# Splitting the filler between two transpose turns of an attention kernel: half a value product and half a projection piece in every step

## The chip, the cores and the metric

The program runs on one core of a Trainium2 chip. The time is the device time of one execution in microseconds (us); lower is better. Traces come from one profiled execution.

## What is computed

Two layers over x of shape 8 x 512 x 32 x 32, each added to its input. Only the first one is touched by the change. Cut to what matters:

```python
xs = group_norm(x).reshape(b, c, seq).transpose(0, 2, 1)      # 1024 pixels, 512 channels
qkv = xs @ Wqkv + bqkv
q, k, v = heads(qkv)                                          # 8 heads of 64
scores = einsum('bhqd,bhkd->bhqk', q, k) / sqrt(64)
attn = softmax(scores)
out = einsum('bhqk,bhkd->bhqd', attn, v)
x = x + (out.reshape(b, seq, c) @ Wout + bout)
```

The second layer (deformable attention in windows of 8 x 8 pixels) works on the result.

## The kernel before, in words

Every engine's program is written out by hand in its order, with semaphores between them. The outer loop goes over the 8 images (`i`). Inside it the attention of the first layer is cut into 32 steps (`n`, `STEPS`): four pairs of heads (`PAIRS`) times eight tiles of 128 queries (`KT`). Work of the second layer for the image before is spread over some of the steps; the rest of it, the output projection and so on follow behind step 31.

In step n TensorE (PE) does this, in this order:

1. `scores(n + 1)` (line 647): 12 matmuls of 64 rows x 512 columns, three products of the high and low halves of q and k for two heads side by side. They need the exponentials of step n to have freed both score banks.
2. `turn(n, 0)` (line 663): 8 transposes of the first head's exponentials into the banks `TB`, which ScalarE (ACT) then copies to `exps_turned` (line 1097).
3. a filler: a value product or a projection piece.
4. `turn(n, 1)`: 8 transposes of the second head's, which VectorE (DVE) copies (line 1425). They wait until ACT has emptied `TB`.

The filler is what the change touches. `value_product(u, half, i)` (line 678) multiplies the turned exponentials of two steps with the values into the bank `OB`; two halves of 16 matmul instructions each in the trace, of 128 rows x 64 columns of weights, two heads side by side. `keep_output` (ACT, line 1201) copies `OB` away. `piece(n, i)` (line 618) computes 512 columns of the next pair's q or k into the bank `MB` with 12 matmuls of 128 rows x 128 columns of weights; ACT (`high_piece`, line 1077) and DVE (`low_piece`, line 1409) split it into halves in `QK`. There are 12 pieces for each image, for n = 0, 2, ..., 22. Their weights stand in a ring of two slots, `wqk_ring`, which the DMA queue of SyncE refills (`load_wq`, line 461) behind the transfers of the reciprocals.

The filler before: step 0 and all odd steps up to 21 hold a whole piece; even steps from 2 to 20 hold a whole value product; steps 22 to 31 hold half a product each.

ACT does in a step: `copy_turned(n)`, the two exponentials of step n + 1 (line 1087), and `keep_output` or `high_piece` if there is one. DVE does two row maxima (line 1416), `copy_turned`, and `low_piece` if there is one. Between them they also hold small work of the second layer; at n = 4 ACT computes a logarithm, for which it loads another table, and loads the table of the exponential again in step 5.

Of the kernel before, what the change touches and what calls it, by code (L numbers as in the profile page):

```python
# [14 lines left out]
CT = C // P  # L15
# [20 lines left out]
def piece_of(n):  # L36
    p, j = n // KT + 1, n % KT
    return (p, j // 2) if p < PAIRS and j % 2 == 0 else None
# [39 lines left out]
def build(nc, x, wqkv, bqk, bv, wo0, bo0, lnw, lnb, lnwt, lnbt, wqT, wkT, wvT, woT, bo1, dww, dwb, pwT,  # L78
          w1T, b1, w2T, b2, w3c, b3, c_ident, c_gavg, c_gxy, c_grid, out):
    with ExitStack() as ctx:  # L80
# [3 lines left out]
        def sem(name):  # L84
            return ctx.enter_context(nc.semaphore(name))

        def at(name, shape, offset, dt=F32):
            return nc.alloc_sbuf_tensor_at(name, shape, dt, offset=offset)
# [44 lines left out]
        WQ = at("wqk_ring", [P, 2, 2, CT, P], AT_WQ, F32R)  # L133
# [82 lines left out]
        MB = PS[:, 7]  # L216
# [64 lines left out]
        piece_full = sem("piece_full")  # L281
# [88 lines left out]
        def wait_after(eng, s, count):  # L370

            if count > 0:
                eng.wait_ge(s, count)
# [223 lines left out]
        def _(pe):  # L597
# [17 lines left out]
            def project_halves(dst, weights, c, ks):  # L615
                for k in ks:
                    for a, half in ((0, XH), (0, XL), (1, XH)):
                        mm = pe.matmul(dst, weights[:, a, k], half[:, k, c:c + 512], start=(k == 0 and a == 0 and half is XH),  # L618
                                       stop=(k == CT - 1 and a == 1))
                return mm  # L620
# [46 lines left out]
            def value_product(u, half, i):  # L667
                p = u // 4
                if half == 0:
                    pe.wait_ge(t_free[0], i * STEPS + 2 * u + 2)  # L670
                    pe.wait_ge(t_free[1], i * STEPS + 2 * u + 2)
                    wait_after(pe, ob_kept, i * (OUTS - 1) + u)
                    if u == 0 and i:
                        pe.wait_ge(off_done, i)
                for kt in range(4 * half, 4 * half + 4):
                    for h in range(2):
                        hc = (2 * p + h) * D
                        mm = pe.matmul(OB[D * h:D * h + D, 0:256], V[:, kt, hc:hc + D], PT[:, u % 2, h, kt],  # L678
                                       start=(kt == 0), stop=(kt == KT - 1))
                if half == 1:  # L680
                    mm.then_inc(av_full, 1)
# [9 lines left out]
                                       skip_group_check=True)  # L691
                mm.then_inc(rbc_full, 1)

            def piece(n, i):
                p, which = piece_of(n)
                w, c = which // 2, 512 * (which % 2)
                pe.wait_ge(wq_in[w], 16 * (PAIRS * i + p))
                wait_after(pe, piece_free, (i * 3 + p - 1) * PIECES + which)
                if n == 0 and i >= 2:
                    pe.wait_ge(o1c_done, i - 1)  # L700
                project_halves(MB, WQ[:, w], c, range(CT)).then_inc(piece_full, 1)

            def group_sums(k, dst, after=0):
                pe.wait_ge(gn_in, k)
# [52 lines left out]
            def turn_sampled(f, j):  # L757
                pe.wait_ge(kvt_done, 2 * j + f + 1)
                turn_rows().then_inc(kv_full, 1)
# [205 lines left out]
            for i in range(B):  # L965
                for n in range(STEPS):
                    if n + 1 < STEPS:
                        scores(n + 1, i)
                    turn(n, 0, i)
                    if n == 0:  # L970
                        piece(0, i)
                    if n >= 2 and n % 2 == 0:
                        value_product(n // 2 - 1, 0, i)
                    if (2 <= n < 22 and n % 2 == 0) or (n > 22 and n % 2):
                        value_product(n // 2 - 1, 1, i)
                    if piece_of(n + 1):
                        piece(n + 1, i)
                    if i + 1 < B and n == STEPS - 1:
                        values(0, i + 1)
                    if i and n == 25:  # L980
                        turn_sampled(0, i - 1)
                    if i and n == 26:
                        turn_sampled(1, i - 1)
                    if i and n == 28:
                        turn_similarities(0, i - 1)
                    if i and n == 29:
                        turn_similarities(1, i - 1)
                    turn(n, 1, i)
                    if i and n == 1:
                        offsets(i - 1)  # L990
                    if i and n == 23:
                        turn_weights(i - 1)
                    if i and n == 24:
                        sample(0, i - 1)
                    if i and n == 25:
                        sample(1, i - 1)
                    if i and n == 26:
                        sampled_keys(i - 1)
                    if i + 1 < B and n == 26:
                        group_sums(2 * i + 2, GSO)  # L1000
                    if i and n == 27:
                        similarities(0, i - 1)
                    if i and n == 28:
                        similarities(1, i - 1)
                    if i and n == 30:
                        sampled_values(i - 1)
                spread_recips(i)
                for half in range(2):
                    value_product(OUTS - 1, half, i)
                if i + 1 < B:  # L1010
                    values(1, i + 1)
                pe.wait_ge(wo0_in, 16 * (i + 1))
                for t in range(CT):
                    project(("o0", t, i), WO0, P * t, OTH, OTL, needs=attended if t == 0 else None)
                if i + 1 < B:
                    values(2, i + 1)
                group_sums(min(2 * i + 3, 2 * B), GSM, i)
                if i + 1 < B:
                    values(3, i + 1)
                if i:  # L1020
                    mlp(i - 1, i)
                else:
                    for n in range(4):
                        pixels(n, i)
                    first_pair(0, 1)
                    first_pair(1, 1)
                    channel(0, i)
                for t in range(1, CT):
                    channel(t, i)
                if i:  # L1030
                    turn_bias(i - 1)
                queries(i)
                if i:
                    if i + 1 < B:
                        first_pair(0, i + 1)
                    attend(i - 1)
                    if i + 1 < B:
                        first_pair(1, i + 1)
                    apply_values(i - 1)
                    for t in range(3):  # L1040
                        output(t, i - 1)
                if i + 1 < B:
                    scores(0, i + 1)
                if i:
                    output(3, i - 1)
# [20 lines left out]
        def _(act):  # L1066
# [173 lines left out]
            for i in range(B):  # L1240
                for h in range(2):
                    exp(0, h, i)
                for n in range(STEPS):
                    if i + 1 < B and n == 22:
                        next_image(i + 1)
                    if i and n in (25, 26):
                        keep_sampled(n - 25, i - 1)
                    if i and i + 1 < B and n == 26:
                        act.dma_start(WV[:].bitcast(F32), wv_dram).then_inc(wv_in, 16)
                    if i and n in (28, 29):  # L1250
                        keep_similarities(n - 28, i - 1)
                    copy_turned(n, i)
                    if n + 1 < STEPS:
                        for h in range(2):
                            exp(n + 1, h, i)
                    if (2 <= n < 22 and n % 2 == 0) or (n > 22 and n % 2):
                        keep_output(n // 2 - 1, i)
                    if i + 1 < B and n in (27, 28):
                        x_high(2 * (n - 27), i + 1)
                        x_high(2 * (n - 27) + 1, i + 1)  # L1260
                    if n == 0:
                        high_piece(0, i)
                    if piece_of(n + 1):
                        high_piece(n + 1, i)
                    if i and n == 0:
                        gelu(i - 1)
                    if i and n == 1:
                        tanh(i - 1)
                    if i and n == 4:
                        log(i - 1)  # L1270
                    if not i and n in (4, 10):
                        wo_high(n // 10)
# [662 lines left out]
```

## Time and profile before

| what | value |
|---|---|
| median of 3 runs | 3384.9 us (3383.76 to 3387.4) |
| profiled execution, its own time | 3384.37 us |
| its span in the trace | 3382.4 us |
| PE busy | 3177.9 us (94%) |
| DVE busy | 2276.8 us (67%) |
| ACT busy | 1689.2 us (50%) |

Times in the trace count from the start of the span. An instruction of TensorE has two records, the weight load (PEld) and the matmul (PE). Matmuls overlap and their ends are modelled, so the distance from start to start tells how long a group took; a busy PE can hide a short gap between two groups.

### The profile page before, as it was taken

The page shows a single profiled execution, that of the slowest core. Times are in us where ns is not written, and L with a number is a line of the kernel's source. Part 1 is how long each engine was busy: PE and PEld are TensorE (multiplying, and loading weights), DVE is VectorE, ACT ScalarE, POOL GpSimd, SP SyncE. Part 2 cuts the span into 40 slices and gives each one's busy share as a digit, 9 for nine tenths or more (in the row PEclk, how much of TensorE's full clock was granted, in tenths as well). Part 3 has the DMA queues.
Part 4 walks back from the last instruction along what each step waited for, and adds up shares of the span by engine and source line. Part 5 has one row for each costly group of instructions (what it writes and reads, how often), then busy time and mean ns, then how long its engine had stood idle before and what let it go on. Part 6 is the DMA issues. An engine that isn't in the chain of part 4 may idle for free.

```text
span 3382.4 us, 51739 instructions
## 1 busy us (share of the span) xinstructions
PE 3177.9 (94%) x20704; PEld 2250.2 (67%) x20704; DVE 2276.8 (67%) x3031; ACT 1689.2 (50%) x2500; POOL 220.9 (7%) x165
## 2 busy tenths in 40 slices
PE   6999699999999999999999999999999999998978
PEld 5767576657766677666776567675776757765545
DVE  5666567677676676776666866668667576666765
ACT  2553455364553655444653645537455364553533
POOL 0000020000100020000200002000020000200200
PEclk9999899999999999999999999999999999998979
DMA  5222012301133111321123111221113311103121
GB/s 180 66 79 80 14 38 76 118 32 43 34 76 113 38 39 40 108 74 53 32 59 99 55 63 31 67 98 39 64 34 79 97 49 48 34 11 118 38 59 50
DMA packets 132158, 213.24 MB, mean 63 GB/s; under 512 B 76561, under 2 KB 95508, under 8 KB 128052
## 3 DMA queue, kind: packets, MB, share of 16 engines
q1 hardware_dynamic: 127252, 182.68, 17.4%
q10 hardware_dynamic: 4672, 27.26, 2.7%
q8 instruction: 168, 2.75, 0.5%
q14 instruction: 66, 0.54, 0.1%
HBM read 162.40 MB, written 47.50 MB: 62 GB/s over the span
## 4 chain that ended last, share of the span: by engine, by line
PE 79%; DVE 11%; ACT 4%; issue 3%; DMA 2%; SPq 0%; another core or an unknown queue 0%; POOL 0%; DVEq 0%; ACTq 0%
PE banks L663 13%; PE banks L678 13%; PE banks L647 11%; PE banks L618 9%; PE banks L608 8%; PE banks L719 4%; PE banks L850 4%; PE banks L860 3%; PE banks L851 3%; PE banks L852 3%; ACT exps L1087 2%; DVE qk_halves L1592 2%; PE banks L926 2%; PE banks L823 2%; DVE neg_max L1416 1%
## 5 line engine op out<-in xcount | busy, mean ns | idle before, releaser
L1416 DVE TENSOR_REDUCE neg_max<-banks 128x1 f32<-128x1024 f32 x512 | 601.6, 1216 | 70.4 <-PE banks L647 68.3
L1425 DVE COPY exps_turned<-banks 128x1024 f32<-128x1024 f32 x256 | 313.5, 1224 | 496.8 <-PE banks L663 488.9
L1087 ACT ACTIVATE exps<-banks,neg_max 128x1024 f32<-128x1024 f32 x512 | 565.0, 1112 | 152.6 <-DVE neg_max L1416 151.3
L1097 ACT ACTIVATE exps_turned<-banks 128x1024 f32<-128x1024 f32 x256 | 262.4, 1025 | 685.9 <-PE banks L663 685.8
L663 PE MATMUL banks<-ident,exps 128*128 128x128 f32 x4096 | 552.3, 278 | 42.7 <-DVE exps_turned L1425 41.9
L663 PEld LDWEIGHTS banks<-ident,exps 128*128 128x128 f32 x4096 | 449.1, 141 | 197.6 <-issue 156.1
L678 PE MATMUL banks<-exps_turned,values 128*64 128x256 f32 x4096 | 483.3, 386 | 6.2 <-issue 6.2
L647 PE MATMUL banks<-qk_halves 64*128 64x512 f32 x3072 | 428.1, 410 | 52.3 <-ACT exps L1087 43.9
L678 PEld LDWEIGHTS banks<-exps_turned,values 128*64 128x64 f32 x4096 | 284.1, 137 | 156.6 <-issue 37.2
L647 PEld LDWEIGHTS banks<-qk_halves 64*128 64x128 f32 x3072 | 280.4, 186 | 137.3 <-issue 99.5
L1592 DVE SCALAR_TENSOR_TENSOR qk_halves<-banks,qk_halves 128x1024 fp32r<-128x1024 f32 x256 | 301.8, 1219 | 70.0 <-ACT qk_halves L1134 69.8
L618 PE MATMUL banks<-x_hi,wqk_ring 128*128 128x512 f32 x992 | 337.2, 403 | 0.0
L1134 ACT ACTIVATE qk_halves<-banks 128x1024 fp32r<-128x1024 f32 x256 | 249.2, 1022 | 143.9 <-PE banks L831 143.7
L850 PE MATMUL banks<-qk_halves,mlp_w_hi 128*128 128x512 f32 x512 | 233.7, 456 | 20.0 <-ACT exps L1150 13.8
L1608 DVE TENSOR_SCALAR exps<-banks,mlp_b 128x512 f32<-128x512 f32 x256 | 190.4, 746 | 33.7 <-PE banks L852 27.0
L618 PEld LDWEIGHTS banks<-x_hi,wqk_ring 128*128 128x128 f32 x992 | 186.6, 188 | 38.3 <-issue 1.7
L850 PEld LDWEIGHTS banks<-qk_halves,mlp_w_hi 128*128 128x128 f32 x512 | 98.5, 192 | 168.5 <-ACT exps L1150 117.8
L851 PE MATMUL banks<-qk_halves,mlp_w_hi 128*128 128x512 f32 x512 | 206.4, 403 | 0.0
L852 PE MATMUL banks<-qk_halves,mlp_w_lo 128*128 128x512 f32 x512 | 205.4, 401 | 0.0
L618 PE MATMUL banks<-x_lo,wqk_ring 128*128 128x512 f32 x496 | 193.8, 391 | 0.0
L1150 ACT ACTIVATE exps<-banks,mlp_b 128x512 f32<-128x512 f32 x256 | 168.1, 693 | 32.6 <-PE banks L852 32.4
L719 PE MATMUL banks<-wv_halves,x_hi 128*128 128x512 f32 x512 | 162.7, 399 | 10.6 <-DVE x_lo L1387 10.6
(189 smaller groups left out, 3899.6 us busy)
## 6 DMA issues: line engine op xcount, KB each, us to landing
wo_halves<-wo_split_dram SPq DMA_DIRECT2D x16, 2048.0 KB, 7.8
wqk_ring<-wqk_split SPq DMA_DIRECT2D x62, 512.0 KB, 4.3
exps_turned<-in_x SPq DMA_DIRECT2D x32, 512.0 KB, 5.3
x_dram<-exps SPq DMA_DIRECT2D x32, 512.0 KB, 2.6
exps_turned<-x_dram SPq DMA_DIRECT2D x32, 512.0 KB, 5.7
out<-exps_turned SPq DMA_DIRECT2D x32, 512.0 KB, 2.6
recips_b<-recips_dram SPq DMA_DIRECT2D x240, 64.0 KB, 3.8
x_image<-in_x ACTq DMA_DIRECT2D x14, 1024.0 KB, 14.4
```

Of the source, the lines that this page charges most:

```text
L618: mm = pe.matmul(dst, weights[:, a, k], half[:, k, c:c + 512], start=(k == 0 and a == 0 and half is XH), stop=(k == CT - 1 and a == 1))
L647: mm = pe.matmul(slot(("s", 2 * n + h, i))[:, 512 * c:512 * c + 512], QK[rows, p % 2, a, P * j:P * j + P], QK[rows, p % 2, b, 512 * c:512 ...
L663: mm = pe.transpose(TB[:, kt // 4, kt % 4 * P:kt % 4 * P + P], PB[:, 2 * h + n % 2, kt * P:(kt + 1) * P], IDENT[:])
L678: mm = pe.matmul(OB[D * h:D * h + D, 0:256], V[:, kt, hc:hc + D], PT[:, u % 2, h, kt], start=(kt == 0), stop=(kt == KT - 1))
L719: mm = pe.matmul(slot(("v", n, i))[:, 512 * s:512 * s + 512], half[:, k, P * tt:P * tt + P], WV[:, a, k], start=(k == 0 and half is XH and ...
L850: pe.matmul(h2_bank(c), W2H[:], h1_hi_half(u)[:, cols], start=True, stop=False)
L851: pe.matmul(h2_bank(c), W2H[:], h1_lo_half(u)[:, cols], start=False, stop=False)
L852: pe.matmul(h2_bank(c), W2L[:], h1_hi_half(u)[:, cols], start=False, stop=True)\
L1087: freed(act.activation(PB[:, 2 * h + n % 2], slot(("s", m, i)), ACT.Exp, bias=NM[:, m:m + 1], accum_out=SS[:, m:m + 1]), ("s", m, i))
L1416: dve.tensor_reduce(NM[:, m:m + 1], slot(("s", m, i)), AX.X, ALU.max, negate=True).then_inc(mx, 1)
L1425: dve.tensor_copy(PT[:, n // 2 % 2, 1, :, P * j:P * j + P], TB.rearrange("p s (k q) -> p (s k) q", k=4)).then_inc(t_free[1], 1)
L1592: freed(dve.scalar_tensor_tensor(out=h1_lo_half(u), in0=slot(("h1", u, j)), scalar=0.0, in1=h1_hi_half(u).bitcast(F32), op0=ALU.max, op1=A ...
```

## The change

Every step from 3 on holds half a value product (even steps the first half, odd ones the second), and every step from 2 to 21 also half a projection piece: even steps begin the piece for n + 2, odd steps end the one for n + 1. Step 1 still holds a whole piece, and so does step 0. Steps from 22 on are as they were. `keep_output` moves with the second half of the product, from even steps to odd ones.

```diff
-            def piece(n, i):
+            def piece(n, i, parts=(0, 1)):
                 p, which = piece_of(n)
                 w, c = which // 2, 512 * (which % 2)
+                if parts == (1,):
+                    project_halves(MB, WQ[:, w], c, range(2, CT)).then_inc(piece_full, 1)
+                    return
                 pe.wait_ge(wq_in[w], 16 * (PAIRS * i + p))
                 wait_after(pe, piece_free, (i * 3 + p - 1) * PIECES + which)
                 if n == 0 and i >= 2:
                     pe.wait_ge(o1c_done, i - 1)
-                project_halves(MB, WQ[:, w], c, range(CT)).then_inc(piece_full, 1)
+                if parts == (0,):
+                    project_halves(MB, WQ[:, w], c, range(2))
+                else:
+                    project_halves(MB, WQ[:, w], c, range(CT)).then_inc(piece_full, 1)
...
                     if n >= 2 and n % 2 == 0:
                         value_product(n // 2 - 1, 0, i)
-                    if (2 <= n < 22 and n % 2 == 0) or (n > 22 and n % 2):
+                    if n >= 3 and n % 2:
                         value_product(n // 2 - 1, 1, i)
+                    if n >= 2 and piece_of(n + 2):
+                        piece(n + 2, i, (0,))
                     if piece_of(n + 1):
-                        piece(n + 1, i)
+                        piece(n + 1, i, (0, 1) if n == 1 else (1,))
...
-                    if (2 <= n < 22 and n % 2 == 0) or (n > 22 and n % 2):
+                    if n >= 3 and n % 2:
                         keep_output(n // 2 - 1, i)
```

On TensorE, in the first image, an even and an odd step of before (line 663 are the turns, 678 the value product, 618 the piece, 647 the scores; a row of 678 counts each of its matmuls once, the trace twice):

```order
L663 MATMUL banks<-ident,exps 128x128 x8
L678 MATMUL banks<-exps_turned,values 64x256 x16
L663 MATMUL banks<-ident,exps 128x128 x8
L647 MATMUL banks<-qk_halves 128x512 x12
L663 MATMUL banks<-ident,exps 128x128 x8
L618 MATMUL banks<-x_hi,wqk_ring 128x512
L618 MATMUL banks<-x_lo,wqk_ring 128x512
L618 MATMUL banks<-x_hi,wqk_ring 128x512 x2
L618 MATMUL banks<-x_lo,wqk_ring 128x512
L618 MATMUL banks<-x_hi,wqk_ring 128x512 x2
L618 MATMUL banks<-x_lo,wqk_ring 128x512
```

The same engine and steps of the changed kernel, one whole step from its first turn to the next scores:

```order
L663 MATMUL banks<-ident,exps 128x128 x8
L678 MATMUL banks<-exps_turned,values 64x256 x8
L618 MATMUL banks<-x_hi,wqk_ring 128x512
L618 MATMUL banks<-x_lo,wqk_ring 128x512
L618 MATMUL banks<-x_hi,wqk_ring 128x512 x2
L618 MATMUL banks<-x_lo,wqk_ring 128x512
L618 MATMUL banks<-x_hi,wqk_ring 128x512
L663 MATMUL banks<-ident,exps 128x128 x8
L647 MATMUL banks<-qk_halves 128x512 x12
```

Both the even and the odd step read so now: 8 of the 16 product matmuls and 6 of the 12 of the piece stand between the two turns, and the engine goes from the product straight to the piece.

On ACT, before, an even step and an odd one (1097 the copy of the turned exponentials, 1087 the exponentials, 1201 `keep_output`, 1077 `high_piece`):

```order
L1097 ACTIVATE exps_turned<-banks 128x8x128
L1087 ACTIVATE exps,exp_sums<-banks,neg_max 128x1024 x2
L1201 ACTIVATE attended<-banks 128x256
L1097 ACTIVATE exps_turned<-banks 128x8x128
L1087 ACTIVATE exps,exp_sums<-banks,neg_max 128x1024 x2
L1077 ACTIVATE qk_halves<-banks,b_qk 128x512
```

And with the change (8 lines further down in the file):

```order
L1105 ACTIVATE exps_turned<-banks 128x8x128
L1095 ACTIVATE exps,exp_sums<-banks,neg_max 128x1024 x2
L1105 ACTIVATE exps_turned<-banks 128x8x128
L1095 ACTIVATE exps,exp_sums<-banks,neg_max 128x1024 x2
L1209 ACTIVATE attended<-banks 128x256
L1085 ACTIVATE qk_halves<-banks,b_qk 128x512
```

`keep_output` now stands in the odd step, ahead of `high_piece`.

## Rows read from the trace of the kernel before

**Rows 1.** The page, busy time, share of the span and instructions.

```profile
PE 3177.9 (94%) x20704; PEld 2250.2 (67%) x20704; DVE 2276.8 (67%) x3031; ACT 1689.2 (50%) x2500; POOL 220.9 (7%) x165
```

**Rows 2.** Stretches of image 3: steps 2-21, 18, 19, 5, 22.

```profile
core 0: us, PE busy (x) PEld busy (x) DVE busy (x) ACT busy (x) POOL busy (x), PEclk, DMA share, GB/s
1215.95:1352.08 136.13, 134.94 (x1000) 99.99 (x1000) 87.09 (x113) 77.48 (x125) 20.31 (x16) 1.00 0.13 33
1325.10:1332.35 7.25, 7.25 (x62) 5.00 (x62) 4.14 (x4) 3.86 (x7) 0.00 (x0) 1.00 0.04 2
1332.35:1338.59 6.24, 6.24 (x42) 4.98 (x41) 3.98 (x5) 3.53 (x6) 0.00 (x0) 1.00 0.10 21
1236.65:1244.14 7.49, 6.31 (x41) 5.00 (x41) 6.62 (x11) 5.94 (x9) 0.00 (x0) 1.00 0.28 91
1352.08:1358.12 6.04, 5.59 (x45) 3.87 (x45) 4.55 (x5) 3.48 (x6) 0.00 (x0) 1.00 0.37 32
```

**Rows 3.** Timeline of PE, steps 18 and 19: start, us, line, operation.

```profile
1325.10 1.67 PE L647 MATMUL banks<-qk_halves 64*128 64x512 f32 x12
1326.70 1.09 PE L663 MATMUL banks<-ident,exps 128*128 128x128 f32 x8
1327.72 3.67 PE L678 MATMUL banks<-exps_turned,values 128*64 128x256 f32 x32
1331.32 1.09 PE L663 MATMUL banks<-ident,exps 128*128 128x128 f32 x8
1332.35 1.66 PE L647 MATMUL banks<-qk_halves 64*128 64x512 f32 x12
1333.93 1.09 PE L663 MATMUL banks<-ident,exps 128*128 128x128 f32 x8
1334.78 0.48 PE L618 MATMUL banks<-x_hi,wqk_ring 128*128 128x512 f32 x1
...
1337.62 1.03 PE L663 MATMUL banks<-ident,exps 128*128 128x128 f32 x8
1338.59 0.74 PE L647 MATMUL banks<-qk_halves 64*128 64x512 f32 x4
```

**Rows 4.** Timeline of PE, step 22 and the start of step 23.

```profile
1352.08 1.67 PE L647 MATMUL banks<-qk_halves 64*128 64x512 f32 x12
...
1354.70 1.95 PE L678 MATMUL banks<-exps_turned,values 128*64 128x256 f32 x16
1356.58 1.09 PE L663 MATMUL banks<-ident,exps 128*128 128x128 f32 x8
1358.12 1.66 PE L647 MATMUL banks<-qk_halves 64*128 64x512 f32 x12 [0.45 <-issue]
```

**Rows 5.** Timeline of PE, step 31: half product, then values of the next image.

```profile
1418.58 1.95 PE L678 MATMUL banks<-exps_turned,values 128*64 128x256 f32 x16
1420.46 0.74 PE L719 MATMUL banks<-wv_halves,x_hi 128*128 128x512 f32 x2
...
1421.95 0.61 PE L719 MATMUL banks<-wv_halves,x_hi 128*128 128x512 f32 x2
```

**Rows 6.** Timeline of ACT in step 5 of image 3.

```profile
1240.41 1.28 ACT L1087 ACT_TABLE_LOAD   x1
...
1243.80 0.20 ACT L1087 ACTIVATION_READ_ACCUMULATOR exps<-banks,neg_max 128x1 f32 x1
1243.89 0.69 ACT L1077 ACTIVATE qk_halves<-banks,b_qk 128x512 fp32r<-128x512 f32 x1
```

**Rows 7.** The instructions on the ring of weights: its loads, issue to landing.

```profile
DMA to landing us min/median/max: 3.1/4.3/13.6
```

**Rows 8.** Timeline of SyncE's queue and of PE in image 4, steps 5 and 6.

```profile
1644.96 0.58 SPq L461 DMA_DIRECT2D wqk_ring<-wqk_split  x1
1650.91 1.66 PE L647 MATMUL banks<-qk_halves 64*128 64x512 f32 x12 [1.19 <-ACT exps L1087]
```

**Rows 9.** Step 31 of image 2, its half product, as a stretch.

```profile
1009.71:1013.01 3.30, 3.30 (x17) 1.54 (x17) 0.13 (x1) 1.02 (x1) 0.00 (x0) 0.56 0.09 30
```

## The prediction

> **What bounds the kernel now.** I read the page first. TensorE is busy for 94% of the span, DVE and ACT far less [rows 1]. Then I cut the trace at the starts of the score groups, which gives the length of each step, and asked for the engines' busy time in these stretches. In image 3, steps 2 to 21 take 136.13 us and TensorE is busy for 134.94 of them; step 18, with a whole value product, takes 7.25 us and step 19, with a whole piece, 6.24, and in both TensorE is busy throughout [rows 2]. All images show these two lengths. A step with half a product and nothing else takes 6.04 us and has 0.45 us of idle time before its next scores [rows 4]: that is the time in which ACT and DVE can turn a step around. Both step lengths in question are above it. So steps 2 to 21 are bound by what TensorE issues, and not by the loop of scores, maxima, exponentials and copies. One step is an exception: step 5, 7.49 us with only 6.31 busy [rows 2], because ACT loads the table of the exponential again (1.28 us) before its exponentials; they end at 1243.80 + 0.20, and the next scores start at 1244.14 [rows 2, 6].
>
> Where PE is busy throughout, the question is what its groups cost, each from its start to the start of the next. The timeline gives it [rows 3]:
>
> - scores to turn: 1326.70 - 1325.10 = 1.60
> - turn to product: 1.02; turn to piece: 1334.78 - 1333.93 = 0.85
> - whole product to turn: 1331.32 - 1327.72 = 3.60
> - piece to turn: 1337.62 - 1334.78 = 2.84
> - second turn to scores: 1.03 after a product, 0.97 after a piece
>
> The reader is to see that the same 8 transposes cost 0.17 us more when a product follows than when a piece follows. Weights of the turns and of the piece fill 128*128 of the array, those of the product 128*64, those of the scores 64*128. Each change of this form costs something, and turn to piece is not such a change.
>
> **The change, part by part.** No matmul is added or removed: 32 product instructions and 12 of the piece for each pair of steps, before and after. What changes is the number of changes of form. Before, an even step has four (scores, turn, product, turn, scores) and an odd one two; with the change each step has four, since product to piece is one and piece to turn is none. That is two more for each pair of steps, in 10 pairs and 8 images.
>
> *Second product group:* two halves in place of a whole. A half costs 1356.58 - 1354.70 = 1.88 [rows 4] and the same before a group of form 128*128 with 512 columns: 1420.46 - 1418.58 = 1.88 [rows 5]. So 2 x 1.88 - 3.60 = +0.16.
> *Turn to product in the odd step too:* 1.02 - 0.85 = +0.17.
> *The piece in two parts:* six instructions of the same shape behind a half product take 1421.95 - 1420.46 = 1.49 [rows 5], two times that is 2.98, against 2.84: +0.14.
> *Second turn behind a piece in both steps:* 0.97 in place of 1.03: -0.06.
> Sum +0.41 a pair. Added up as a whole step, 1.60 + 1.02 + 1.88 + 1.49 + 0.97 = 6.96, a pair 13.92 against 13.49, +0.43; the difference is rounding, and I take 0.42, so 6.955 a step.
>
> The Trainium skill has the rule behind this, in "TensorEngine Tiling (Array Packing)", section Key Properties: changing the tiling mode drains TensorE. It speaks against the change and gives no figure; the rows bear it out, with about 0.2 us for each change (0.42 for two more). By the view that only matmuls count, the pair would stay at 13.49.
>
> *Step 5* stays at 7.49, set by ACT, as its own TensorE work of 6.96 is still below it. So here the longer filler costs nothing, while step 4 gets shorter. In an image, steps 2 to 21 become 20 x 6.955 + (7.49 - 6.955) = 139.6, against 136.13: +3.5. Image 0 has no such table load but other waits of the kind; I take it as equal. 8 x 3.5 = +28.0 us.
>
> *Waits that come with it, even steps:* the first half of a piece now needs `MB` and its weights at 1.60 + 1.02 + 1.88 = 4.50 us into an even step, where before they were needed 1.60 + 0.85 = 2.45 us into the odd step behind it. `MB` is freed by `low_piece`, behind DVE's copy of the step before. All five DVE instructions of step 19 take 3.98 us [rows 2], and this one stands second of those that come after the turn; it is done before 4.50, and I cost it at nothing. If that cover were gone, everything behind it on TensorE (second turn, next scores) would move, one for one.
> *The ring of weights:* this cover is thinner. In image 4, a load is issued at 1644.96 and step 6 starts at 1650.91 [rows 8]. Now it is wanted at 1650.91 + 4.50 = 1655.4; with the median landing of 4.3 it lands at 1649.3, with the longest of 13.6 [rows 7] at 1658.6: 3.2 us late. Before, it was wanted at 1650.91 + 7.25 + 2.45 = 1660.6, and even the longest was in time. 4 loads an image are of this kind. At best none is late (0), at worst a few of the 32 are late by some 3 us (10 us). Since the median is 6 us early, the value is nearer to the lower end: +4.
> *`keep_output`* moves to odd steps, between the exponentials and `high_piece`. ACT is busy for 3.86 and 3.53 us in steps of 7.25 and 6.24 [rows 2], so it has room; the next product starts in the next even step, 2.6 us after its scores, and these already need the exponentials that stand before `keep_output`. Nothing.
> *Steps 0, 1 and 22 to 31 and all behind them* are untouched. TensorE's clock matters at one place there: the half product of step 31 took 3.30 us in image 2 at a granted clock of 0.56 [rows 9], against 1.88 in image 3 [rows 5], the engine having waited just before it. Where the low stretch (1.2 of 2.4 GHz) falls can move with the rest; each gained or lost is 1.4 us, and I count none, some 6 us for the range.
>
> **The sum.** 3384.37 (the profiled execution's own time; its span is 3382.4) + 28.0 + 4 = 3416.4. The median of the runs is 3384.9, 0.5 above, within their own spread. I say 3416.
>
> **The rivals.**
>
> *The even filler removes a wait (faster).* The idea: a step with a short filler is bound by the others' loop, one with a long filler by TensorE, and the mean of both fillers is better than their alternation. For it speaks that the odd step, 6.24, is only 0.20 above the loop of 6.04. The mechanism decides from the point where a short step is longer than its TensorE work; the saving is then what it waits. If TensorE's busy time hid 0.3 us of such a wait in each odd step, and the changes of form were free besides, a pair would be 13.19: 80 x -0.3 = -24, 3360 us. Against it: 6.24 of 6.24 busy, and turn to piece, piece to turn add up without a gap. Chance 0.04.
>
> *Nothing happens.* The groups' overlap hides the changes of form when the groups are small. Then only step 4 against 5 counts; 7.25 and 7.49 become 6.75 and 7.49: 8 x -0.5 = -4, and with the ring's +4 it is 3384. Against it are the half products of rows 4 and rows 5, which show the 0.08 each. Chance 0.04.
>
> *A new wait in the even step.* `MB` or the ring is late not now and then but each time, as the first half piece is wanted a step earlier. At 0.5 us for each of the 80 even steps it is +40 on top of 28: 3453; if only the ring's loads are later than I take, with 10 to 20 us in place of 4, 3422 to 3432. For it speaks the landing of up to 13.6; against it 3.98 before 4.50 and the median landing. It begins where a load takes more than 10.4 us from its issue (1655.4 - 1644.96). Chance 0.10.
>
> *As worked out:* 0.82, with its own range from 3404 (no late load, 6 us less by the clock, 0.35 a pair) to 3428 (10 us of late loads, 6 of the clock).
>
> **How the numbers follow.** 3403 to 3430 holds the likely case and the milder part of the third rival; outside it lie the first two rivals (0.08) and the harder part of the third, so about 0.15 in all. A measurement of this kernel tells some 0.2% (7 us) from no change. Slower by more than that: 0.82 + 0.10 = 0.92. Within: 0.05, the second rival and the edge of the first. Faster: 0.03.
>
> **What the profile of the changed kernel would show.** Step lengths from scores to scores of 6.95 us, even and odd alike, in steps 2 to 21 but for step 5 near 7.5; each made of 1.60, 1.02, 1.88, 1.49 and 0.96. The same counts of matmuls; TensorE still busy throughout. No wait before the first half piece but in a few steps, where a load of the ring landed late; these would show as idle time of PE ended by the ring's DMA. Steps 22 to 30 as before. I am wrong if the even step waits for `low_piece` throughout, if product to piece costs less than the 0.08 and 0.07 that the halves show, or if odd steps come out under 6.9.

## The result, and the profile after

The changed kernel takes 3428.05 us (median of 6 runs, 3418.51 to 3438.74); the kernel before, in the runs beside it, 3386.15 (3382.19 to 3390.82). The ratio is 1.0122, with a 95% interval of 1.0099 to 1.0145: the change makes the kernel slower by 1.2%. The profiled execution took 3424.17 us (span 3422.2), 39.8 more than the profiled one of before.

The page shows the same number of matmuls, and TensorE busy for 3218.4 us where [rows 1] had 3177.9, 40.5 more; the other engines' busy times hardly differ:

```profile
PE 3218.4 (94%) x20704; PEld 2249.2 (66%) x20704; DVE 2280.8 (67%) x3031; ACT 1687.0 (49%) x2500; POOL 221.7 (6%) x165
```

The busy time of the engines in stretches of image 3, cut again at the starts of the score groups: steps 2 to 21 together, then steps 18, 19, 5 and 22. They answer to [rows 2, 4]. Step 2 is among them: it too holds half a product and half a piece now.

```profile
core 0: us, PE busy (x) PEld busy (x) DVE busy (x) ACT busy (x) POOL busy (x), PEclk, DMA share, GB/s
1229.48:1371.86 142.38, 139.20 (x1000) 99.26 (x1000) 87.81 (x113) 77.45 (x125) 20.43 (x16) 1.00 0.12 32
1344.05:1351.00 6.95, 6.95 (x51) 4.95 (x50) 4.15 (x4) 3.21 (x5) 0.00 (x0) 1.00 0.00 0
1351.00:1357.96 6.96, 6.96 (x53) 4.96 (x52) 3.98 (x5) 4.15 (x7) 0.00 (x0) 1.00 0.09 19
1250.34:1257.84 7.50, 7.02 (x51) 4.98 (x51) 5.92 (x11) 5.71 (x9) 0.00 (x0) 1.00 0.31 91
1371.86:1377.90 6.04, 5.59 (x45) 3.85 (x45) 4.56 (x5) 3.21 (x5) 0.00 (x0) 1.00 0.28 29
```

Steps 18 and 19, 7.25 and 6.24 before, are now 6.95 and 6.96, and TensorE is busy in all of both. Step 5 is 7.50 and step 22 is 6.04, as before. But the 20 steps take 142.38 us with 139.20 busy: 3.2 us are idle, where before 1.2 were (7.49 - 6.31 in step 5). Of these 3.2, step 5 has 0.5, so 2.7 lie elsewhere. The timeline of TensorE shows step 18 by its groups, beside [rows 3]:

```profile
1344.05 1.66 PE L647 MATMUL banks<-qk_halves 64*128 64x512 f32 x12
1345.64 1.09 PE L663 MATMUL banks<-ident,exps 128*128 128x128 f32 x8
1346.66 1.95 PE L678 MATMUL banks<-exps_turned,values 128*64 128x256 f32 x16
1348.54 0.50 PE L618 MATMUL banks<-x_hi,wqk_ring 128*128 128x512 f32 x1
...
1350.04 1.04 PE L663 MATMUL banks<-ident,exps 128*128 128x128 f32 x8
1351.00 0.50 PE L647 MATMUL banks<-qk_halves 64*128 64x512 f32 x2
```

From start to start: 1.59 scores, 1.02 turn before a product, 1.88 half product, 1.50 half piece, 0.96 second turn: 6.95. The same timeline in step 14 of the same image shows the gap:

```profile
1316.08 1.95 PE L678 MATMUL banks<-exps_turned,values 128*64 128x256 f32 x16
1320.73 0.50 PE L618 MATMUL banks<-x_hi,wqk_ring 128*128 128x512 f32 x1 [2.70 <-DMA wqk_ring<-wqk_split]
```

The half product would have made room for the half piece at 1316.08 + 1.88 = 1317.96; the weights of the ring came at 1320.7. SyncE's queue just before:

```profile
1305.77 1.08 SPq L476 DMA_DIRECT2D recips_b<-recips_dram  x2
1306.96 3.12 SPq L485 DMA_DIRECT2D mlp_rows<-attended  x4
1310.13 0.59 SPq L461 DMA_DIRECT2D wqk_ring<-wqk_split  x1
```

The load was issued at 1310.13, behind the reads of the reciprocals and the four transfers of `rows_to_dram`, 7.8 us ahead of the time at which it was wanted, and took 10.6 us to land.

A late load can cost more than the wait for it. In step 10 of image 5 (2111.05 to 2121.32) TensorE waited for the load as well, and in this step the granted clock is 0.86:

```profile
2117.54 0.50 PE L618 MATMUL banks<-x_hi,wqk_ring 128*128 128x512 f32 x1 [1.93 <-DMA wqk_ring<-wqk_split]
...
2111.05:2121.32 10.27, 8.35 (x51) 5.88 (x50) 4.47 (x5) 3.21 (x5) 0.00 (x0) 0.86 0.06 14
```

The first matmul comes 2.0 us late, but the step is 3.32 us longer than 6.95, and step 11 behind it (clock 0.96) is 0.27 longer. In image 3 the engine waited longer, 2.7 us, and the clock in that step stayed at 1.00; so a wait doesn't bring a low clock each time.

**Where the 39.8 us are**, from the lengths of all steps in the two traces:

| part | us |
|---|---|
| steps 2 to 21, length of the steps without a late load | +27.1 |
| steps 2 to 21, three steps with a late load, with the low clock in the last (image 0 step 10 +1.85, image 3 step 14 +2.78, image 5 step 10 +3.32) | +7.95 |
| steps 22 to 29 | +3.7 |
| all behind step 30 of the images | +0.6 |

The four numbers sum to 39.4; the other 0.4 lie in the start and in steps 0 and 1. In steps 22 to 29 there are two things. In step 22 of image 5 (7.87 us in place of 6.04) ACT took 2.32 us to issue one of the two loads of the next image; in the kernel before none of the 14 issues took more than 0.49. And step 26 takes 11.27 in place of 9.64 us in images 1 and 5, at a granted clock of 0.85; in the kernel before it is 1.00 in step 26 of every image. Image 0, on the other hand, has 0.7 us less in step 26 than before.

TensorE's busy time in steps 2 to 21 grew by some 4.2 us in each image but image 5 (134.94 to 139.20 in image 3), more than the 3.5 of the steps' length: step 5 is set by ACT, and 0.7 us of its idle time were filled. In image 5 it grew by 5.9, since busy time counts the low clock too.

### The profile page after: what moved, and what is told of

Same layout as the page of the kernel before. It is cut to its first block, busy times and chain, and to the rows that moved or that the text cites. A ratio compares the mean times of both kernels' runs of the same rounds, so it can differ in the third digit from the quotient of the medians.

```text
span 3422.2 us, 51739 instructions
## 1 busy us (share of the span) xinstructions
PE 3218.4 (94%) x20704; PEld 2249.2 (66%) x20704; DVE 2280.8 (67%) x3031; ACT 1687.0 (49%) x2500; POOL 221.7 (6%) x165
## 4 chain that ended last, share of the span: by engine, by line
PE 78%; DVE 11%; ACT 4%; issue 3%; DMA 3%; SPq 0%; another core or an unknown queue 0%; ACTq 0%; POOL 0%; DVEq 0%
PE banks L663 12%; PE banks L678 12%; PE banks L647 10%; PE banks L618 10%; PE banks L608 8%; PE banks L725 4%; PE banks L856 4%; PE banks L866 3%; PE banks L857 3%; PE banks L858 3%; DVE qk_halves L1600 2%; PE banks L932 2%; PE banks L829 2%; ACT exps L1095 2%; DVE neg_max L1424 1%
## 5 line engine op out<-in xcount | busy, mean ns | idle before, releaser
L663 PEld LDWEIGHTS banks<-ident,exps 128*128 128x128 f32 x4096 | 457.7, 142 | 178.3 <-issue 154.5
L678 PE MATMUL banks<-exps_turned,values 128*64 128x256 f32 x4096 | 503.7, 389 | 6.2 <-issue 6.2
L618 PE MATMUL banks<-x_hi,wqk_ring 128*128 128x512 f32 x992 | 361.8, 415 | 6.4 <-DMA wqk_ring<-wqk_split 6.4
L856 PE MATMUL banks<-qk_halves,mlp_w_hi 128*128 128x512 f32 x512 | 233.9, 457 | 20.3 <-ACT exps L1158 13.5
L725 PE MATMUL banks<-wv_halves,x_hi 128*128 128x512 f32 x512 | 161.7, 397 | 10.6 <-DVE x_lo L1395 10.6
```

The costliest lines, as they stand in the source:

```text
L663: mm = pe.transpose(TB[:, kt // 4, kt % 4 * P:kt % 4 * P + P], PB[:, 2 * h + n % 2, kt * P:(kt + 1) * P], IDENT[:])
L725: mm = pe.matmul(slot(("v", n, i))[:, 512 * s:512 * s + 512], half[:, k, P * tt:P * tt + P], WV[:, a, k], start=(k == 0 and half is XH and ...
L856: pe.matmul(h2_bank(c), W2H[:], h1_hi_half(u)[:, cols], start=True, stop=False)
```

## Experiments

The theory A to be tested: each change of the weights' form on TensorE (128*128, 128*64 or 64*128 of the array) costs about 0.2 us, the change adds two for each pair of steps, and that is 27 us; what is beyond is loads of the ring that are wanted earlier than before, and come late. Rival B: it is the cutting into halves that costs (fill, new banks, more groups), or the new order of product and piece, whatever the forms. Rival C: the loads of the ring are all there is to the even steps' growth.

**The ring's load ahead of the reciprocals.** On the kernel after:

```diff
                 for u in range(OUTS - 1):
+                    if u in (1, 3, 5, 7):
+                        load_wq(4 + u // 2, i)
                     recips_around(u, i)
...
-                    if u in (1, 3, 5, 7):
-                        load_wq(4 + u // 2, i)
```

> The changed kernel, with the four loads of the ring of weights of each image issued one transfer of reciprocals earlier (ahead of it in SyncE's queue in place of behind it), some 10 us. Theory A (the loss is the changes of form on TensorE, about 28 us, and on top of it loads of the ring that land late, 8 us in the profile of the changed kernel and more in its slower runs): the step lengths stay at 6.95, no wait for the ring is left, the time is 3384.4 + 28 = 3412 to 3416 and the runs lie closer together than 3418 to 3439. Rival B (the late loads are a by-product and something else spreads the runs): time and spread as in the changed kernel, about 3428.

Measured: 3416.38 us (3414.77 to 3422.41), with 3412 to 3416 expected, beside 3393.54 of before on the same chip, 1.0069 (1.0057 to 1.0082). The 62 loads still take up to 13.6 us. The view of all that touches `wqk_ring` has no transfer any more among what TensorE waited for. In the kernel after it had 6 such waits, 14.2 us: 3 late loads, each counted at a matmul and at a weight load.

```profile
L461 SPq DMA_DIRECT2D wqk_ring<-wqk_split x62: 319/583/2821, 45.5 to 2967.8; - x62
its engine sat idle before it (us, times) until:
  issue: 64.4, 172
...
DMA to landing us min/median/max: 3.1/4.5/13.6
```

In images 2 to 4 the load is now issued 22 to 26 us ahead of its use, in place of 6.7 to 11.6. Steps 2 to 21 are +26.9 us against before, all at 6.95 (but for step 5, and step 11 of image 0). So the ring's part goes away with the early load, and the 27 us stay: C falls.

**The same pair side by side on a second chip**, since the result's 1.0122 and this 1.0069 were not measured beside each other. The kernel after, unchanged:

> The changed kernel itself, beside the kernel before and the other three on one chip. Theory A: even and odd steps of 6.95, one to five waits for the ring of weights in the even steps 6, 10, 14 and 18, of 1 to 4 us each; 30 to 45 us above the kernel before.

3438.23 us (3429.7 to 3444.52), 1.0135 (1.0113 to 1.0156). With the early load:

> The changed kernel with the ring's loads issued ahead of a transfer of reciprocals, once more, now beside the changed kernel itself. Theory A: no wait for the ring, 27 us of longer steps left; 20 to 30 us above the kernel before, and 8 to 18 us below the changed kernel. Rival B (the ring's loads are no cause of their own): within 4 us of the changed kernel.

3419.41 us (3415.69 to 3422.99), 1.0080 (1.0066 to 1.0094): 19 us below, on one chip (4 runs of each, whose ranges don't meet). In the trace of the unchanged kernel the same view of the ring's loads reads

```profile
  DMA wqk_ring<-wqk_split: 28.0, 12
...
DMA to landing us min/median/max: 3.1/4.7/13.8
```

and steps 2 to 21 are +47.4 us against before, of which 27 are the steps' length and 20.3 late loads and what follows them: six steps wait for a load (one to five were expected), in images 0, 1, 3, 4 and 5, and the longest takes 12.20 us in place of 6.95. TensorE's matmuls wait 12.6 us for loads in all. Most of the other 7.7 goes with a lower granted clock: four of the six steps, and the step behind one of them, have 0.79 to 0.89 in place of 1.00. With the early load no step from 2 to 21 has a lower clock, and these steps are +26.8. The two traces of the kernel after have three and six late loads. That this number changes between executions would explain why its runs spread over 20 and 15 us, and those with the early load over 8 and 7; it was not counted in the runs without a trace.

**The same edit of the load, on the kernel before:**

> The kernel before, with the ring's loads issued early in the same way. Theory A: in the kernel before even the longest landing (13.6 us) is in time, so nothing is gained: within 3 us of the kernel before. Rival B (loads issued early help in any case, by another order in SyncE's queue): faster by 8 us or more.

3389.90 us (3385.6 to 3398.59) beside 3391.27, 0.9999 (0.9989 to 1.0010). A load took up to 14.5 us there, and none was late. The early load gives nothing by itself; it takes back what late loads had added to the changed kernel. Expectation and prediction both say that in the kernel before even the longest landing is in time. That is so at step 6 of image 4, but in the trace of before the load of step 10 of image 0 was issued only 10.0 us ahead of its use, and that of step 14 of image 1 10.3. They landed after 7.5 and 4.0; with 13.6 they would have been late.

**Product in halves, piece whole.** On the kernel after:

```diff
-                    if n >= 2 and piece_of(n + 2):
-                        piece(n + 2, i, (0,))
                     if piece_of(n + 1):
-                        piece(n + 1, i, (0, 1) if n == 1 else (1,))
+                        piece(n + 1, i)
```

> One part of the change alone: the product is held in halves by even and odd steps, but the piece stays whole in the odd step. Theory A: the even step has 1.60 + 1.02 + 1.88 + 1.03 = 5.53 us of TensorE work, which is below the 6.04 that the loop of maxima, exponentials and copies takes, so it takes 6.04 and waits 0.5; the odd step takes 1.60 + 1.02 + 1.88 + 2.87 + 0.97 = 8.34. A pair 14.38, 80 x 0.89 = +71 us, about 3455. Rival D (unequal steps cost nothing, as the loop has slack elsewhere): 5.53 + 8.34 = 13.87, as the changed kernel, about 3416.

One run, 3457.79 us, where about 3455 was expected. Busy times of an odd and an even step of it:

```profile
1365.94:1374.25 8.31, 8.31 (x57) 6.19 (x57) 3.52 (x5) 4.18 (x7) 0.00 (x0) 1.00 0.13 16
1374.25:1380.32 6.07, 5.58 (x45) 3.85 (x45) 4.60 (x5) 3.21 (x5) 0.00 (x0) 1.00 0.01 3
```

The even step has only 5.58 us of matmuls and takes 6.07, with its next scores waiting for the exponentials:

```profile
1380.32 0.96 PE L647 MATMUL banks<-qk_halves 64*128 64x512 f32 x6 [0.49 <-ACT exps L1093]
```

Here is the loop of scores, maxima, exponentials and copies that the prediction gave 6.04 us. No even step of 2 to 21 goes below 6.03, and what the odd step gets on top adds in full. Of the divisions that were run this is the one in which an uneven filler has a price, and the kernel before was not it: its short step, 6.24, was above the loop.

**Three changes of form in place of four.** On the kernel with the early load, the half product of steps 2 to 21 goes behind the second turn, so that turn, half piece, turn stand together:

```diff
                     turn(n, 1, i)
+                    if 2 <= n < 22:
+                        value_product(n // 2 - 1, n % 2, i)
```

with the two calls between the turns kept for n >= 22 alone.

> As the run before it, but in steps 2 to 21 the half product stands behind the second turn, just ahead of the next scores, and only the half piece stands between the turns. Every step holds the same matmuls as in the changed kernel, but changes the form of the weights three times in place of four (scores to turn, turn to product, product to scores; the piece has the turns' form), six for a pair, as many as the kernel before. Theory A (each change of form costs about 0.2 us): steps of 1.60 + 0.85 + 1.46 + 0.97 + 1.88 = 6.76, a pair 13.52 against 13.49 of before, the time within 4 us of the kernel before (3382 to 3390). Rival C (what costs is that the groups are smaller, or that each step has both fillers): steps stay at 6.95 and the time at 3412 or more. A wait of the second turn for ACT's copy would show as longer steps too: by the rows it is done 2.2 us after the first turn starts, and wanted at 2.31.

3404.79 us (3401.0 to 3411.17), 1.0035 (1.0023 to 1.0048), 11 us above before where at most 4 were expected. The step's length came as expected and the total did not. TensorE's timeline of a step:

```profile
1327.40 1.65 PE L647 MATMUL banks<-qk_halves 64*128 64x512 f32 x12
1328.98 1.09 PE L663 MATMUL banks<-ident,exps 128*128 128x128 f32 x8
1329.83 0.48 PE L618 MATMUL banks<-x_hi,wqk_ring 128*128 128x512 f32 x1
...
1331.31 1.04 PE L663 MATMUL banks<-ident,exps 128*128 128x128 f32 x8
1332.28 1.95 PE L678 MATMUL banks<-exps_turned,values 128*64 128x256 f32 x16
1334.16 1.21 PE L647 MATMUL banks<-qk_halves 64*128 64x512 f32 x8
```

6.76 us, as worked out, with both the product and the piece in halves and the same matmuls. The pair is 13.54 against 13.49 before and 13.91 in the kernel after; steps 2 to 21 of all images together are 1.1 us *below* before. (Step 4 got shorter while step 5 is still set by ACT.) So halves have hardly a price in themselves, 0.05 us a pair, and B's first half falls. What makes this kernel slower than before lies elsewhere: in its trace steps 22 to 29 are +22.7 us. ACT's timeline in step 22 of image 3, and the stretches of steps 22 and 23:

```profile
1356.20 4.10 ACTq L1228 DMA_DIRECT2D x_image<-in_x  x2
1360.40 1.02 ACT L1107 ACTIVATE exps_turned<-banks 128x1024 f32<-128x1024 f32 x1 [4.84 <-issue]
```

```profile
1354.48:1363.71 9.23, 5.62 (x46) 3.85 (x45) 4.05 (x4) 4.17 (x7) 0.00 (x0) 1.00 0.44 31
1363.71:1371.35 7.64, 7.58 (x49) 5.62 (x50) 3.40 (x6) 3.37 (x6) 0.00 (x0) 0.78 0.70 258
```

ACT issues the two loads of the next image for 4.1 us; its copy of the turned exponentials is behind them, TensorE waits for that (5.62 of 9.23 busy), and in the step behind, the granted clock is 0.78 and the step takes 7.64 in place of 6.07. It happened in three of the seven images (3.69 us the longest single issue), and the low clock in step 23 in two of these. Step 22 of the three is 8.1 us longer in all and step 23 3.1; step 26 of images 3, 4 and 5 has the low clock (11.27 in place of 9.64), 4.9 in all. The rest is in images 0 (+4.0, with step 26 at a clock of 0.73) and 7 (+3.0).

**The same, with that issue placed behind the exponentials.** On top of the last one:

```diff
-                    if i + 1 < B and n == 22:
-                        next_image(i + 1)
...
                             exp(n + 1, h, i)
+                    if i + 1 < B and n == 22:
+                        next_image(i + 1)
```

> The kernel with three changes of form in each step and the ring's loads early, with one more edit: ACT issues the load of the next image in step 22 behind its copy and exponentials in place of ahead of them. In its last profile that kernel won 1 us against the kernel before in steps 2 to 21 and lost 23 in steps 22 to 29: in images 3, 4 and 5 the issue took 2.5 to 3.7 us in place of 0.5 while the copy waited behind it, and stretches of low clock fell into steps 23 and 26. Theory A: with the issue behind ACT's urgent work, step 22 is 6.04 in all images, low clock in step 23 is gone, and the time comes within 5 us of the kernel before on the same chip. Rival E (the low clock in steps 22 to 29 comes by itself, from where the images' lengths put it): step 22 is 6.04, but steps 23 or 26 keep their longer forms, and the time stays 5 to 10 us above. Either way there is no clear gain on the kernel before.

3387.76 us (3383.17 to 3398.11) beside 3390.92, 0.9993 (0.9981 to 1.0006): no difference from before. ACT's timeline:

```profile
1355.44 1.02 ACT L1107 ACTIVATE exps_turned<-banks 128x1024 f32<-128x1024 f32 x1 [1.64 <-PE banks L663]
1356.36 1.11 ACT L1097 ACTIVATE exps<-banks,neg_max 128x1024 f32<-128x1024 f32 x1
1356.89 1.71 ACTq L1228 DMA_DIRECT2D x_image<-in_x  x2
```

The issue now lies beside the exponential, and step 22 takes 6.03 to 6.05 in all images. The low clock in step 23 is gone as well. But step 26 still has a granted clock of 0.85 in images 1, 2 and 6 (11.25 to 11.27 us), and steps 22 to 29 are +6.0 in the trace: rival E was right about step 26. Its 5 to 10 us in the total did not come. So with halves, three changes of form a step, early loads and the later issue, the even filler costs nothing that the runs tell from before, and brings nothing. No version that I ran is faster than before.

**One more change of form in the kernel before, with the piece untouched.** The second half of the product goes behind the second turn in the even steps:

```diff
-                    if (2 <= n < 22 and n % 2 == 0) or (n > 22 and n % 2):
+                    if n > 22 and n % 2:
                         value_product(n // 2 - 1, 1, i)
...
                     turn(n, 1, i)
+                    if 2 <= n < 22 and n % 2 == 0:
+                        value_product(n // 2 - 1, 1, i)
```

> The kernel before, with one edit: in the even steps 2 to 20 the second half of the value product stands behind the second turn in place of ahead of it. Pieces, and the work of each step, are as before; the even step has five changes of form in place of four. Theory A: even steps take 1.60 + 1.02 + 1.88 + 1.03 + 1.88 = 7.41 in place of 7.25, odd ones 6.24 as before; 80 x 0.16 = +13 us, 3397 to 3400. Rival C (groups that hold both fillers cost, a change of form is free): 3384, no change. A gain would mean that the copies of ACT and DVE were late for the turns before.

3413.30 us (3408.29 to 3416.16), 1.0054 (1.0040 to 1.0068).

```profile
1339.62 1.66 PE L647 MATMUL banks<-qk_halves 64*128 64x512 f32 x12
1341.22 1.09 PE L663 MATMUL banks<-ident,exps 128*128 128x128 f32 x8
1342.24 1.95 PE L678 MATMUL banks<-exps_turned,values 128*64 128x256 f32 x16
1344.12 1.09 PE L663 MATMUL banks<-ident,exps 128*128 128x128 f32 x8
1345.14 1.95 PE L678 MATMUL banks<-exps_turned,values 128*64 128x256 f32 x16
```

The even step is 7.39 (expected 7.41), the odd one 6.26: a product in halves with a turn between them costs 0.14 to 0.16 us more than whole, with all else as before. That is what A gives, and the price is on TensorE. The total was expected at +13 and measured at +20, which is a miss. In image 0 the steps 5, 6, 11 and 12 grew (8.28 and 8.95 in place of some 7.25), 5.5 us of the 17.6 in steps 2 to 21. At the end of step 5 TensorE waits 1.95 us for the exponentials, where before 0.94: ACT's `keep_output` has to wait for the moved half, and both it (101.81 in place of 100.97) and the exponentials (107.49 in place of 106.65) come 0.84 us later. In the steps behind (6 and 12) the granted clock is 0.81. And step 26 of images 2 to 6 fell in a low clock. One of them, from this kernel's trace, and the same stretch from the kernel before:

```profile
1393.00:1404.20 11.20, 8.78 (x77) 5.96 (x66) 7.81 (x21) 3.81 (x6) 0.00 (x0) 0.85 0.69 241
```

```profile
1378.66:1388.30 9.64, 7.22 (x62) 5.45 (x58) 7.89 (x20) 3.81 (x6) 0.00 (x0) 1.00 0.64 221
```

A granted clock of 0.85 in place of 1.00, and 1.6 us more.

**Piece ahead of product.** On the kernel with the early load, the two lines of the piece stand ahead of those of the product, so that the changes of form are as many (four a step) but in another order.

> The changed kernel with early loads of the ring and, in steps 2 to 21, the half piece ahead of the half product. Four changes of form as in the changed kernel (scores to turn, piece to product, product to turn, turn to scores). Theory A: steps of 6.95 as there, within 0.05, and no wait. If it is the step from product to piece that costs and not any change of form, the steps come out near 6.76.

One run, 3405.30 us. From start to start a step is 1.59 scores, 0.84 turn, 1.57 half piece, 1.88 half product, 1.02 second turn: 6.90. The order of product and piece is worth 0.05 us a step; the four changes keep the rest (6.76 with three). B's second half falls too, except for these 0.05. By these two kernels the fourth change costs 0.14 us, by the changed kernel and the one with three 0.19. What in the change of form takes this time, no run takes apart.

## Why the prediction came out as it did

**The step lengths: right, and not by luck.** Predicted 6.955 even and odd, step 5 at 7.49; measured 6.95 and 7.50, by 1.59, 1.02, 1.88, 1.50 and 0.96 in place of 1.60, 1.02, 1.88, 1.49 and 0.97. The sum over steps 2 to 21 is 27.1 us of the +28.0 foretold; image 0, which the prediction took as equal, got 2.6 without its late load, as its steps 5 and 11 were bound by others before and got no longer. The experiments bear out the reason: one change of form more (+0.14 in the even step), four a step (6.95, 6.90 in the other order), three a step (6.76). Two more changes for each pair of steps are 0.37 us of the pair's 0.42 (13.91 - 13.54); the halves by themselves, without more changes, are the other 0.05.

The Trainium skill states, in "TensorEngine Tiling (Array Packing)", section Key Properties, that changing the tiling mode drains TensorE. The runs agree that such a change costs time, with (13.91 - 13.54) / 2 = 0.19 us for each of the two changes by which a pair differs between the kernels with four and three a step; the draining itself is in no row.

**`MB` and `keep_output` at nothing: right.** No even step waits as such; step 18 is 6.95 of 6.95 busy.

**The ring at +4: the term that was too small.** It measured 8.0 us in the profiled execution (8.2 with the step behind), and on the second chip 19 between the medians with and without early loads. The step that failed: "4 loads an image are of this kind", with the margin of the load of step 6 of image 4 (10.4 us from issue to use, which the trace of after confirms) for all of them. The four aren't alike. The load of step 14 stands behind `rows_to_dram` on SyncE's queue, and is issued 6.3 to 10 us ahead of its use; in image 0 the load of step 10 has 5.5. With the longest landing of before, 13.6 us, such a load comes 4 to 8 us late and not 3.2, and shorter landings are late too: the two with short leads landed after 7.2 and 10.6 us. The third late load, in step 10 of image 5, is of the kind that the prediction had in mind, with 10.7 us ahead and 12.6 to land. In the trace of before the load of step 14 already had a shorter lead than those of steps 6 and 10 in images 2 to 4 (12.4 to 12.8 us to its use, 15.0 to 16.5 at step 6 and 14.7 to 15.6 at step 10). The term also had nothing for the granted clock behind a late load: 1.3 of the 3.3 us of step 10 of image 5, and most of 7.7 beyond 12.6 us of waits on the second chip. The rival "if only the ring's loads are later than I take", 3422 to 3432, had priced this, and the median of 3428.05 lies there; of the likely case only its upper end (3428) reaches it. So the stated range held thanks to this rival, which had a share in a chance of 0.10, and the forecast of 3416 was 12 us low. The likely case's lower end is also a slip: at 0.35 a pair and 6 us less by the clock its own terms give 3401 and not 3404, which changes nothing here.

**What the prediction did not have at all:** ACT's issue of the next image's loads, 2.32 us in place of 0.49 in one image (1.8 us here, but 8.1 us in the version with three changes of form, and 3.1 more by the clock in the step behind).

**The clock at +-6: right in size, wrong in place.** 3.3 us in step 26 of two images and 1.6 behind the late load of image 5 (which is in the ring's sum above), 4.9 together; the part behind step 30 differs by +0.6 in all. The prediction looked for it in step 31 and put 1.4 us to each; it came in step 26 with 1.6. That it came as a loss was a chance that the prediction left open.

**The rivals.** That the even filler removes a wait fell: the odd step lost nothing but went from 6.24 to 6.95 with TensorE busy. That nothing happens fell with the same rows. The wait that comes each time did not come.

## What to carry to other kernels

Before work is spread evenly over steps, look whether the short step is above the loop of the other engines: if TensorE is busy in all of both, evenness gives nothing, and every group that is cut in two between groups of another weight form costs one or two changes of form, of 0.14 to 0.19 us each in this kernel. If a cut is wanted, put groups of one form side by side.

Work that is moved a step earlier takes its transfers' margins with it. Count for each of the loads, not for one of them, what is issued ahead of it on its queue and how long there is from issue to use, and hold that against the longest landing in the trace and not the median; moving the issue earlier is a few lines. The longest differed between traces (12.3 to 15.5 us here), so leave some room above it.

## What the runs showed of the hardware that was not expected

- A load of the ring of 512 KB lands after 3.0 to 3.1 us at best, 4.0 to 4.7 in the median and 12.3 to 15.5 at worst, 62 loads in each of eleven traces. In the two traces of the kernel after, with leads of 4.8 to 11.7 us, 9 of the 64 loads that the change concerns were late. In the five traces with early loads on top of the change, with leads of 16 us and more, none was.
- Behind a wait of TensorE for a late load, the granted clock was lower in five of nine cases (0.79 to 0.86 over the step; in these two traces all other steps from 2 to 21 have 1.00, but for the step behind such a wait in image 5), and the step grew by 1.3 us or more beyond the wait. A wait of 2.7 us went without it (image 3 of the kernel after), one of 2.0 us did not (image 5).
- The issue of a transfer on ACT's queue, 0.45 us in the median and at most 0.49 in the kernel before, took 2.3 to 3.7 us in one to three images of some of the others (the kernel after, both traces of that with the early load, that with three changes of form; not the kernel after on the second chip). Where computing was queued behind it, it was held for as long. The write of the reciprocals to DRAM was issued 4.3 to 4.5 us ahead of it there rather than 3.8. But so it was in most images of the same traces in which the issue took 0.49, and in all of the kernel after on the second chip, so this distance alone is not the cause. The cause stays open; only that the longer issue costs nothing behind the exponentials was shown.
- Stretches of low granted clock fell in other places from kernel to kernel: on step 26 in none of images 1 to 6 of before, in two of after, in five of the kernel with one more change of form, 1.6 us each, with step 26 itself unchanged. Differences of some 5 to 8 us between two kernels' traces come from that alone here.
